# Local attention on one NeuronCore: the value products of heads 0 to 3 issued directly in front of those of heads 4 to 7, at the end of a tile's slot on the tensor engine

## What is computed

```python
h = shift_token(x)
q, k, v = split(h @ wqkv)                       # 8 heads of 64
q, k = rotary_xpos(l2norm(q) * qs, l2norm(k) * ksc)
# windows of 64 tokens; a query sees its own window and the one before
sim  = einsum('bhwid,bhwjd->bhwij', bq, bk)     # masked outside the band
attn = softmax(sim)
out  = einsum('bhwij,bhwjd->bhwid', attn, bv)   # the value products
x = x + out @ wo
x = x + gelu_ffn(layernorm(shift_token(x)))
```

## Time and profile before

| | us |
|---|---|
| median of three timed runs (range) | 3087.51 (3085.33 to 3089.71) |
| the profiled execution, its own time | 3090.91 |
| span of the profiled execution | 3089.1 |
| PE busy in the span | 2833.4 (92%) |
| DVE busy | 2126.4 (69%) |
| ACT busy | 1965.1 (64%) |
| POOL busy | 1086.9 (35%) |

### The profile page before, as it was taken

The page is one execution under the profiler, slowest core; times in us unless marked ns, Lnnn a source line. Parts: engine busy times, 40 slices in busy tenths (PEclk is TensorE's granted clock), DMA queues, the critical chain, the costliest instruction groups (busy, mean ns, idle before and its releaser), DMA issues. The chain is left out here.

```text
span 3089.1 us, 64908 instructions
## 1 busy us (share of the span) xinstructions
PE 2833.4 (92%) x20108; PEld 1808.7 (59%) x20108; DVE 2126.4 (69%) x3716; ACT 1965.1 (64%) x5578; POOL 1086.9 (35%) x1228
## 2 busy tenths in 40 slices
PE   6799899997889689878799999998989999999898
PEld 3577896774654434435466666666435666666643
DVE  4666565665764779666578887886447888788666
ACT  4455564656753744263388888886438888888744
POOL 0233342330000534110155555554225555555431
PEclk9899998997999889899899999999999999999999
DMA  4200120000000000120000000000000000000000
GB/s 138 76 17 21 52 70 22 18 20 7 8 16 0 1 0 1 46 40 1 26 2 0 0 0 0 0 0 19 1 8 2 0 0 0 0 0 0 1 21 35
DMA packets 82995, 51.57 MB, mean 17 GB/s; under 512 B 28848, under 2 KB 75568, under 8 KB 82864
## 3 DMA queue, kind: packets, MB, share of 16 engines
q1 hardware_dynamic: 78768, 41.56, 4.8%
q0 software_dynamic: 4096, 8.40, 0.9%
HBM read 31.59 MB, written 18.35 MB: 16 GB/s over the span
## 5 line engine op out<-in xcount | busy, mean ns | idle before, releaser
L2016 PE MATMUL banks<-weights,hf 128*128 128x512 f32 x768 | 436.5, 652 | 24.5 <-POOL hf L462 11.3
L2150 ACT ACTIVATE probs<-banks,minus_max,rnorm 128x128 f32<-128x128 f32 x1024 | 455.3, 465 | 3.1 <-DVE minus_max L2235 3.1
L2059 POOL TENSOR_TENSOR qk_cross<-qk_raw,rope_scaled 128x512 f32<-128x512 f32 x256 | 325.9, 1274 | 50.9 <-DVE minus_max L2235 33.1
L2215 DVE COPY probs_t<-banks 128x512 f32<-128x512 f32 x256 | 175.9, 687 | 132.6 <-PE banks L1994 132.2
L2069 POOL TENSOR_TENSOR qk_rot<-qk_rot,rnorm 128x512 f32<-128x512 f32 x128 | 133.5, 1043 | 257.9 <-DVE qk_rot L2268 245.6
L834 ACT ACTIVATE probs<-banks,minus_max 128x128 f32<-128x128 f32 (+1 forms) x512 | 208.3, 426 | 17.5 <-DVE minus_max L873 14.5
L2150 ACT ACTIVATION_READ_ACCUMULATOR probs<-banks,minus_max,rnorm 128x1 f32 x1024 | 217.9, 213 | 0.0
L2231 DVE TENSOR_REDUCE minus_raw<-banks 128x8 f32<-128x1024 f32 x128 | 156.7, 1224 | 56.4 <-PE banks L1981 31.9
L2008 PE MATMUL banks<-v_tok,probs_t 128*64 128x64 f32 x3072 | 174.6, 228 | 8.7 <-DVE probs_t L2215 3.8
L2008 PEld LDWEIGHTS banks<-v_tok,probs_t 128*64 128x64 f32 x3072 | 139.3, 137 | 71.4 <-issue 42.5
L2249 DVE TENSOR_REDUCE sumsq<-qk_sq 128x16 f32<-128x1024 f32 x128 | 154.8, 1209 | 27.0 <-issue 19.9
(11 more groups left out here) (357 smaller groups left out, 7118.1 us busy)
## 6 DMA issues: line engine op xcount, KB each, us to landing
sorted_x<-zero_rows SPq DMA_DIRECT2D x10, 512.0 KB
rows_in<-sorted_x SPq DMA_DIRECT2D x18, 256.0 KB, 3.1
sorted_y<-rows_out SPq DMA_DIRECT2D x18, 256.0 KB, 2.4
x_res<-in_x SPq DMA_DIRECT2D x8, 512.0 KB, 6.4
out_x<-x_res SPq DMA_DIRECT2D x16, 256.0 KB, 2.0
w1b<-in_L_ffn_w SPq DMA_DIRECT2D x8, 256.0 KB
s_branch<-in_L_ffn_w SPq DMA_DIRECT2D x8, 256.0 KB
w1g<-in_L_ffn_W SPq DMA_DIRECT2D x8, 256.0 KB, 2.9
```

The lines of the kernel that those rows point to most:

```text
L2016: pe.matmul(ps[:, misc(k, j)], hf[:, n // 2 % 2, 0, n % 2 * P:(n % 2 + 1) * P], wqkv[:, w:w + QW], start=True, stop=True).then_inc(*S[name ...
L2059: return pool.tensor_tensor(by_half(tw[:, n, at]), by_half(qk[:, n, at])[:, :, ::-1, :], tab[:, n, 2 * w + 1].rearrange("p (a d) -> p a d" ...
L2150: last = act.activation(pr[:, k % 2, head], ps[:, 2 * (k % 2) + par, c * P:(c + 1) * P], ACT.Exp, scale=rn[:, k % 4, head:head + 1], bias= ...
L2215: dve.tensor_copy(pt[:, h], ps[:, 4]).then_inc(*S["turned_sb"].inc)
```

## The change

On PE alone, in a slot's list of parts, `pe_mix(.., 0)` leaves its place between the K projection and the second `pe_turn`, and stands directly in front of `pe_mix(.., 1)` as the slot's last part but one. The other engines' queues hold the same instructions in the same order.

```diff
                     if here(i, k + 3):
                         pe_project(pe, i, k, k + 3, K_AT, "k")
                     if here(i, k - 1):
-                        pe_mix(pe, i, k - 1, 0)
                         pe_turn(pe, i, k - 1, 1)
                     if here(i, k + 1):
                         pe_project(pe, i, k, k + 1, V_AT, "v")
...
                         mm.then_inc(*S["ot_ps"].inc)
                     if here(i, k - 1):
+                        pe_mix(pe, i, k - 1, 0)
                         pe_mix(pe, i, k - 1, 1)
```

## The result

The changed kernel takes 3125.22 us (median of four runs, 3121.78 to 3128.25) against 3087.56 for the kernel before in four (3085.33 to 3089.71): 1.0126 of it, 95% interval 1.0113 to 1.0138, or 37.7 us slower. 3130 was forecast, 3114 to 3150 as the range.

The account below looks back on a forecast made before the run. PE's round plus its waits was taken as the bound, with ACT's and DVE's chains nearly equal; 122 full slots x 0.383 = 46.7 us, less 4.8, gave +42 on 3087.5, said as 3130, range 3114 to 3150.

Parts of the forecast that it names:

- The old place gives nothing back: Before the V projection, removing 0.62 us of value products only makes PE wait for ACT's copy of the keys; gain 0.
- The second transposes, moved up, help nobody: They end earlier on PE, but DVE's own queue sets when its second copy reads them; costed at 0.
- A hold of about 0.8 us at the V projection: PE idles 0.82 us in front of the V projection in every slot, until ACT's copy of the keys ends.
- What the new place costs: Attended-row transposes to last value products grows from 0.637 to 1.02 us (0.53 + 0.49), 0.383 us more per tile.
- The wait for DVE vanishes: Last value products no longer wait for DVE's second copy, a mean delay of 0.107 us before.
- The loop's turn: PE's extra 0.17 us before the mask at each hardware-loop turn taken as hidden: 28 x 0.17 = 4.8 us credit.
- Edge slots at 0: The six slots at the ends of the two depths neither gain nor lose time.
- DVE's scaling isn't held: Last value products would end near 1916.33, before DVE's scaling of the attended rows starts at 1916.68, so no wait.
- costlier restart: Rival: step between value products is 0.62, not 0.49, and the loop's turn isn't hidden; 62.6 us, 3150; chance 0.10.
- The clock: Rival: a pause in each slot drops PE's clock to 1.2 GHz, and the time would pass 3200; chance 0.03.
- PE alone: Rival: with the keys copied before PE reaches the V projection, only PE's steps count; 23 us faster, 3064; chance 0.03.

Follow-up runs that it names:

- e1: Kernel before, with the first value products moved only past the second transposes, directly in front of the V projection: 3088.65 us, ratio 0.9999.
- e2: Kernel before, with six of the eight value-product matmuls of heads 0 to 3 left out in every tile: 3088.62 us, ratio 0.9995.
- e5: Changed kernel, with DVE's second copy of the probabilities moved ahead of its two rotary products: 3129.41 us, ratio 1.0135 to the kernel before.
- e6: Kernel before, with DVE's second copy of the probabilities moved ahead of its two rotary products: 3054.03 us, ratio 0.9949 on its chip.
- e3: Changed kernel, with ACT's copies of the keys and of K moved ahead of the four exponentials: 3086.01 us, ratio 0.9989 to the kernel before.
- e8: Changed kernel, with ACT's copies of keys and K ahead of the exponentials and DVE's second copy ahead of its rotary products: 3026.80 us, ratio 0.9857.
- e4: Kernel before, with ACT's copies of the keys and of K moved ahead of the four exponentials: 3068.44 us, ratio 0.9995 on its chip.
- e11: Changed kernel, with only ACT's copy of the keys moved ahead of the four exponentials: 3121.85 us, ratio 1.0101 to the kernel before.
- e7: Kernel before, with ACT's copies of keys and K ahead of the exponentials and DVE's second copy ahead of its rotary products: 3038.06 us, ratio 0.9899.

## Why the prediction was right

- **The old place gives nothing back.** Right, and shown three ways: the V projection stayed 4.06 us behind the Q projection, e1 moved the products within the cover for nothing, and e2 left most of them out for nothing.
- **The second transposes, moved up, help nobody.** Right in the full slots: DVE's second copy starts 3.32 us behind its first (1940.59 to 1943.91), against 3.26 before; its place in DVE's own queue sets it. At the end of a depth it is otherwise (below).
- **A hold of about 0.8 us at the V projection.** Right: reckoned from starts, as it was forecast (0.82), it is 1942.97 - 1941.68 - 0.43 = 0.86; the list's 0.70 counts from the modelled end of the transposes.
- **What the new place costs.** Mechanism right, size a little high. The step from value products to value products was bounded by 0.46 to 0.62 and taken as 0.49. In the slot above, both groups and the step to the mask take 1945.55 - 1944.46 = 1.09, and the step to the mask is 0.62 as before, so the step was 0.47; in other slots 0.46 (1.08). That is 29 ns a row on the mean of 16; the rows start in pairs, one pair each 0.058. It lies between the row's 31 and the 25 that the Trainium skill's page "TensorE: Matmul & The Clock Gate" ("Back-to-back issue gap") lists, as the gap of an isolated matmul, for up to 64 columns; by that figure the forecast would have been 31 us instead of 42, and 38 were measured. At 0.46 instead of 0.49 this term alone is 122 x 0.03 = 3.7 us less. The forecast's lower bound for the step was the right value.
- **The wait for DVE vanishes.** Right (0 of 41 slots), and e5 shows that the copy's time no longer matters.
- **The loop's turn.** Taken as hidden, 0.17 at 14 turns a depth. A loop of 14 rounds branches back 13 times, and both traces show 13 pauses a depth, 26 in all; the slots into the loop and out of it have none. Before, the mask came 0.74 to 0.80 behind the last value products there, and 0.62 elsewhere. Now the distance from the value products to the mask is 1.09 to 1.13 at the turn against 1.08 elsewhere, so up to 0.05 is left: 26 x 0.14 = 3.6 us instead of 4.8. That the pause comes from a queue without instructions in stock is the prediction's inference; the rows show only that it shrinks when the value products are not held (to 0.69 in e6 also).
- **Edge slots at 0.** Not right. In each depth the first tile's slot grew by 0.08, but the last value products, those of the last two tiles, came 1.0 us earlier against the last mask: -0.93 a depth, -1.9 us in all. There DVE's second copy does wait for the second transposes, and these no longer stand behind value products: for the last tile but one of the first depth the copy starts 1.49 behind the first (2150.25 to 2151.74) instead of 2.04 (2132.87 to 2134.91), for the last tile 1.50 instead of 2.05. So the transposes that come earlier do help at a depth's end.
- **DVE's scaling isn't held.** It is, by up to 0.2 us in one slot of four (11 of 41). I see no slot that is longer for it: the steps of PE that are named above account for all four.
- **The rivals.** The costlier restart didn't come. The clock stayed at 1.00 with 0.7 us of standstill in every slot. "PE alone" fails for the reason given, ACT's copy. But its own condition was too weak: in e3 the keys are copied before PE gets to the V projection, and the time is 3086 us and not 3064, since the last value products then wait for DVE. Only with both copies out of the way, in e8, is the new order the faster one, and by 11 us instead of 23.

The sum made again with what was measured: 0.46 + 0.53 - 0.637 = 0.353 a full tile, times 122 is 43.1; less 3.6 for the loop's turns and 1.9 at the edges, 37.6. The two traces differ by 38.0 in local attention. So the forecast was near by its mechanism, and a little nearer by luck: the step and the edges made it 5.6 us too high, and the credit for the turns, itself 1.2 us too high, took some of that back.

## What to carry to other kernels

Work that stands between the release of a copy on another engine and the product which waits for that copy is free up to the length of that engine's chain; the same work one place behind the wait is paid in full, less whatever wait already stood there. Before moving a part, mark in one slot every wait that a queue really meets, with what ends it, and ask on which side of the last one the part will stand. And where two chains are nearly equal, an edit on one may show almost nothing (e4), since the other holds the slot, while both together change even which order of the rest is better: an order should be judged again once the waits around it are gone.

## What the runs showed of the hardware

The V projection is slower in itself when PE has waited for it. Its two rows of 128x512 start 0.53 us apart in all 41 slots of the changed kernel (1942.97 to 1943.50), and 0.43 apart in all 43 of e3, where nothing holds it; so it lasts 1.13 us in the timeline there and 1.02 here. A hold isn't the only thing that does this: the rows of the K projection start 0.51 apart in most slots of every trace, with no hold named, and why is not shown. The transposes behind a hold in e11 take 0.58 to the next part instead of 0.53. Value products show no such cost: the next part follows 0.62 behind them whether DVE's copy held them or not.

So a hold on the V projection costs about 0.1 us more than its length: in e7 the V projection starts 0.08 to 0.16 us earlier against the Q projection than before, and the next part follows it 0.86 instead of 0.96 behind. It doesn't explain e6, which gained 16 us where the holds said 13: there the distance to the last value products falls to 0.53 in all slots, as expected, and the other 3 us are the pause at the loop's turn, 0.79 before and 0.69 in e6. That was read from the rows, not tested by itself.
